# A fused two-layer block: two weight matrices staged in other buffers and loaded later, and one made partly by GpSimd

## The reference

```python
# layer 1, on h = layernorm(x)
h   = rmsnorm(h) * g_res @ W_in + b_in
s   = scan over the context rows: s[i] = a * s[i-1] + c * rmsnorm(ctx[i]) * g_init   # first 512 of 1024 channels
x   = x + h + s[plug]            # plug: one row of s for each token, from the cumulated lengths
# layer 2, on y = layernorm(x)
xr  = mu_r * y + (1 - mu_r) * y_prev ;  xk = mu_k * y + (1 - mu_k) * y_prev
out = x + sigmoid(xr @ W_r.T) * (relu(xk @ W_k.T) ** 2 @ W_v.T)
```

## Time and profile before

| | us |
|---|---|
| median of 3 runs | 780.18 |
| lowest, highest | 779.64, 780.68 |
| profiled execution | 780.35 |
| its span, first to last instruction | 778.8 |
| mean granted TensorE clock | 0.992 |

### The profile page before, as it was taken

How to read it: one execution, slowest core, us unless ns; L and a number is a source line. 1 busy time by engine, 2 the same in 40 slices (tenths; PEclk the granted TensorE clock), 3 DMA queues, 4 the chain that set the end, 5 groups by cost and what they waited for, 6 DMA issues and landing times.

```text
span 778.8 us, 10909 instructions
## 1 busy us (share of the span) xinstructions
PE 755.4 (97%) x3462; PEld 621.9 (80%) x3463; DVE 556.2 (71%) x1005; ACT 413.7 (53%) x682; POOL 175.5 (23%) x175
## 2 busy tenths in 40 slices
PE   7878899999999999999999999999999999999997
PEld 4656688888888888888888888888888888888876
DVE  6797886766858677686776769577676967667552
ACT  4346565554546655455664545556454655544760
POOL 6622131313102131220313122131311213130000
PEclk9999999999999999999999999999999999999999
DMA  8556170524417053350705326071531706140011
GB/s 311 147 192 178 41 215 3 153 105 109 149 42 216 0 128 128 88 169 37 213 7 122 135 69 187 14 194 50 121 135 47 209 0 185 72 108 15 1 54 55
DMA packets 42765, 85.73 MB, mean 110 GB/s; under 512 B 3536, under 2 KB 3536, under 8 KB 42704
## 3 DMA queue, kind: packets, MB, share of 16 engines
q1 hardware_dynamic: 30768, 63.74, 21.8%
q0 software_dynamic: 9216, 16.78, 13.6%
q10 hardware_dynamic: 2736, 4.73, 1.8%
HBM read 64.26 MB, written 21.76 MB: 110 GB/s over the span
## 4 chain that ended last, share of the span: by engine, by line
PE 88%; DVE 4%; DMA 2%; issue 2%; ACT 2%; POOL 1%; SPq 0%; DVEq 0%; ACTq 0%; POOLq 0%
PE bank L494 28%; PE bank L495 28%; PE bank L496 28%; PE bank L599 3%; DMA xt<-in_x_turned 1%; POOL ring L433 1%; DMA s_rows<-scanned 1%; DMA ctx_rows<-in_ctx 1%; DVE ring L1034 1%; DVE xk_lo L908 1%; DVE scratch L1004 0%; DVE gate L1062 0%; ACT scratch L809 0%; DVE bn_a L937 0%; ACT scratch L807 0%
## 5 line engine op out<-in xcount | busy, mean ns | idle before, releaser
L433 POOL DMA_INDIRECT ring<-s_rows,patch_now x60 | 101.7, 1695 | 262.7 <-DMA s_rows<-scanned 231.0
L908 DVE TENSOR_TENSOR xr_lo<-scratch,xr_hi 128x512 fp32r<-128x512 f32 x124 | 85.6, 690 | 70.3 <-ACT xr_hi L715 69.8
L1004 DVE SCALAR_TENSOR_TENSOR scratch<-turned,cols,scratch 128x512 f32<-128x512 f32 x128 | 94.5, 749 | 31.5 <-ACT scratch L764 24.9
L715 ACT ACTIVATE turned<-bank 128x512 f32<-128x512 f32 x64 | 33.2, 604 | 137.1 <-PE bank L599 133.5
L494 PE MATMUL bank<-wi_hi,xt_hi 128*128 128x512 f32 x256 | 102.1, 399 | 3.3 <-DVE xt_lo L908 2.7
L494 PE MATMUL bank<-xk_hi,wk_hi 128*128 128x512 f32 x256 | 100.1, 391 | 3.4 <-DVE xk_lo L908 3.4
L494 PE MATMUL bank<-wr_hi,xr_hi 128*128 128x512 f32 x256 | 99.7, 390 | 1.0 <-DVE xr_lo L908 1.0
L495 PE MATMUL bank<-wi_lo,xt_hi 128*128 128x512 f32 x256 | 100.4, 392 | 0.0
L496 PE MATMUL bank<-wi_hi,xt_lo 128*128 128x512 f32 x256 | 100.2, 391 | 0.0
L496 PE MATMUL bank<-xk_hi,wk_lo 128*128 128x512 f32 x256 | 99.6, 389 | 0.0
L495 PE MATMUL bank<-xk_lo,wk_hi 128*128 128x512 f32 x256 | 99.6, 389 | 0.0
(11 more groups left out here) (134 smaller groups left out, 1283.4 us busy)
## 6 DMA issues: line engine op xcount, KB each, us to landing
ring<-in_x SPq DMA_DIRECT2D x16, 1024.0 KB, 7.4
out<-gate SPq DMA_DIRECT2D x64, 256.0 KB, 2.1
xt<-in_x_turned SPq DMA_DIRECT2D x14, 1024.0 KB, 5.2
ctx_rows<-in_ctx SPq DMA_DIRECT2D x16, 512.0 KB, 8.0
s_rows<-scanned ACTq DMA_DIRECT2D x16, 256.0 KB, 2.4
gate<-in_L_xattn_W_in SPq DMA_DIRECT2D x4, 256.0 KB, 6.2
xt<-in_x_turned SPq DMA_DIRECT2D x2, 512.0 KB, 8.0
ring<-in_x_turned SPq DMA_DIRECT2D x1, 1024.0 KB, 12.9
```

Source lines behind the costliest of these rows:

```text
L433: pool.indirect_dma_start(ring[b.slot][:, t, :], None, s_rows[:, :], bass.IndirectOffsetOnAxis(ap=rows, axis=0), compute_op=ALU.add).then_ ...
L715: return nc.scalar.activation(to, of, ACT.Copy)
L908: return nc.vector.tensor_tensor(to, whole, high, ALU.subtract)
L1004: nc.vector.scalar_tensor_tensor(scratch[:, 2 + i % 2, :], turned[:, c, 1:S + 1], cols[:, 1 + which, c:c + 1], scratch[:, i % 2, :], ALU.m ...
```

## The change

Edits on five engines, all in the opening:

- Staging: W_r into `xt`, W_k into `gate`, W_v into ring buffer 2.
- SP: W_r is loaded once x_lo(0) is whole, W_k once `s_stored` of batch 0 has come, ahead of batch 1's context, and W_v once `s_stored` of batch 1 has come. Guards of the shared buffers follow.
- GpSimd: low parts 0 to 2 of W_k after `root_c(1)`, part 3 after `root_b(0)`; `root_a(1)` ahead of batch 1's gathers; the identity matrix made earlier.
- PE: the first scan after chunk 0 of the first projection; the gate product waits for W_r's low parts one by one.
- ACT: W_k's high parts in iteration -1, ahead of `squares_c(1)`; in iteration 0 `gates` ahead of W_v's high parts, and `squares_c(2)` after `squares(0)`. Two small loads are issued after the averages.
- DVE: no W_k; W_r's low parts between the mixes; `x_lo(1, 1)`, `stats_c(1)` and `scan_input(1)` inside the loop of sums; `norm_b(1)` between `ka_low(0, 1)` and `ka_low(0, 2)`.

```diff
-        staged = [gate, turned[:, :, 1:S + 1], ring[2], gate]
+        staged = [gate, xt, gate, ring[2]]
...
+            reached(sp, xt_lo_ready, Batch(0, 0), 2, 2)
             load_w(WR, w_r)
+
+            reached(sp, s_stored, Batch(0, 0), 16, 16)
+            sp.wait_ge(w_lo_ready[WIN], C)
+            load_w(WK, w_k)
 
             reached(sp, far_over, Batch(0, 0), 1, 1)
             load_ctx(Batch(0, 1))
             rows_added(sp, Batch(0, 0))
             load_x(Batch(0, 1))
-
+            reached(sp, s_stored, Batch(0, 1), 16, 16)
             reached(sp, xt_lo_ready, Batch(0, 1), 2, 2)
-            load_w(WK, w_k)
-            sp.wait_ge(w_lo_ready[WIN], C)
             load_w(WV, w_v)
...
                     reached(sp, xt_lo_ready, new.plus(-1), 2, 2)
+                    if is_first(new, 2):
+                        sp.wait_ge(w_lo_ready[WR], C)
                     load_xt(new)
                     reached(sp, out_ready, b.plus(-1), T, T)
                     if is_first(new, 2):
-                        sp.wait_ge(w_lo_ready[WK], C)
+                        sp.wait_ge(w_lo_ready[WV], C)
                     load_x(new)
...
+            def weight_lo(w, first, last):      # GpSimd
+                for c in range(first, last):
+                    pool.wait_ge(w_hi_ready[w], c + 1)
+                    nc.gpsimd.tensor_tensor(wt_lo[w][:, c, :], staged[w][:, c, :], f32(wt_hi[w][:, c, :]),
+                                            ALU.subtract).then_inc(w_lo_ready[w], 1)
...
+                if is_first(nxt):
+                    weight_lo(WK, C - 1, C)
                 if new.exists(B):
                     far(new)
+                    if is_first(nxt):
+                        root_a(new)
                     add_patches(new)
-                if is_first(nxt):
-                    root_a(new)
...
             root_c(Batch(0, 1))
+            weight_lo(WK, 0, C - 1)
             batches(pool, iteration, B)
...
-                            pe.wait_ge(w_lo_ready[WR], C)
+                            pe.wait_ge(w_lo_ready[WR], c + 1)
...
                 for t in range(T):
                     project_tile(Batch(0, 0), t, c)
-                    if c == 1 and t == 1:
-                        pe.wait_ge(decay_lo_ready, 1)
-                        scan(Batch(0, 0))
                 if c == 0:
                     sum_marks()
+                    pe.wait_ge(decay_lo_ready, 1)
+                    scan(Batch(0, 0))
...
-                        act.wait_ge(w_lo_ready[WV], C)
+                        act.wait_ge(w_lo_ready[WK], C)
...
                     elif is_first(b):                 # ACT, iteration 0
                         mix_hi(b, 0, C)
-                        weight_hi(WK)
                         mix_hi(b, C, 2 * C)
+                        gates(b)
                         weight_hi(WV)
-                        gates(b)
-                        squares_c(new)
...
                 if is_first(b):
                     squares(b)
+                    squares_c(new)
                     u_high(new)
...
                 if is_first(nxt):                     # ACT, iteration -1
                     x_hi(new, 1)
+                    weight_hi(WK)
                     squares_c(new)
...
                 if is_first(nxt):                     # DVE, iteration -1
-                    stats_c(new)
                     for t in range(T):
                         add_x(nxt, t)
                         statistics_b(nxt, t)
+                        if t == 1:
+                            x_lo(new, 1)
+                            stats_c(new)
+                        if t == 2:
+                            scan_input(new)
                     stats_b(nxt, T)
-                    scan_input(new)
                     u_low(new)
                     norm_b(nxt)
+                    weight_lo(WR, 0, 1)
                     scan_out(new)
...
-                if b.exists(B):                       # DVE, iteration 0
+                if is_first(b):
+                    mixing(b, 0, 2)
+                    weight_lo(WR, 1, 2)
+                    mixing(b, 2, 3)
+                    weight_lo(WR, 2, 3)
+                    mixing(b, 3, 4)
+                    weight_lo(WR, 3, 4)
+                    mixing(b, 4, 5)
+                elif b.exists(B):
                     mixing(b, C if is_last(b) else 0, 2 * C if is_last(b) else C + 1)
-                if is_first(b):
-                    weight_lo(WK)
...
+                if nxt.exists(B):
+                    add_x(nxt, 3)
                 if is_first(b):
                     weight_lo(WV)
                 if nxt.exists(B):
-                    add_x(nxt, 3)
                     stats_b(nxt)
                 if is_first(b):
                     ka_low(b, 0)
+                    ka_low(b, 1)
+                    norm_b(nxt)
+                    ka_low(b, 2)
+                    ka_low(b, 3)
                     stats_c(new)
-                    ka_low(b, 1)
                     scan_input(new)
-                    ka_low(b, 2)
                     stats_a(new)
-                    ka_low(b, 3)
                     u_low(new)
-                    norm_b(nxt)
...
-            x_lo(Batch(0, 0), 0)                      # DVE, ahead of the iterations
             dve.wait_ge(cols_loaded, 16)
             dve.wait_ge(w_averaged, 1)
             centre(0)
             centre(1)
+            x_lo(Batch(0, 0), 0)
...
             u_low(Batch(0, 0))
+            x_lo(Batch(0, 0), 1)
             weight_lo(WIN, 2, 3)
             dve.wait_ge(bias_loaded, 16)
             scan_out(Batch(0, 0))
             patches()
-            statistics_a(Batch(0, 0), 0)
-            x_lo(Batch(0, 0), 1)
             weight_lo(WIN, 3, 4)
-            stats_a(Batch(0, 0), 1)
+            stats_a(Batch(0, 0))
...
             x_lo(Batch(0, 1), 0)
-            weight_lo(WR, 0, 2)
-            x_lo(Batch(0, 1), 1)
-            weight_lo(WR, 2, C)
             batches(dve, iteration, B)
```

More of the change, by code:

```diff
@@ L459, in iteration @@
                     root_c(new)
+                if is_first(nxt):
+                    weight_lo(WK, C - 1, C)
                 if new.exists(B):
                     far(new)
+                    if is_first(nxt):
+                        root_a(new)
                     add_patches(new)
-                if is_first(nxt):
-                    root_a(new)
             make_decay(0, P, 0)
             make_blocks()
+            nc.gpsimd.memset(ident[:, :], 0.0).then_inc(ident_ready, 1)
+            pool.wait_ge(ident_ready, 1)
+            nc.gpsimd.affine_select(out=ident[:, :], in_=ident[:, :], compare_op=ALU.not_equal, fill=1.0, base=0,
+                                    pattern=[[-1, P]], channel_multiplier=1).then_inc(ident_ready, 1)
             pool.wait_ge(half_ready, 1)
@@ L471, in _ @@
             make_decay(1, W32, P)
-            nc.gpsimd.memset(ident[:, :], 0.0).then_inc(ident_ready, 1)
-            pool.wait_ge(ident_ready, 1)
-            nc.gpsimd.affine_select(out=ident[:, :], in_=ident[:, :], compare_op=ALU.not_equal, fill=1.0, base=0,
-                                    pattern=[[-1, P]], channel_multiplier=1).then_inc(ident_ready, 1)
             pool.wait_ge(patches_ready, 1)
@@ L818, in turned_out @@
                         reached(act, mix_lo_ready, b.plus(-1), 2 * C, 2 * C)
-                        if is_first(b):
-                            act.wait_ge(w_lo_ready[WR], C)
                     copy(turned[:, :, 1 + t * P:1 + (t + 1) * P],
@@ L869, in _ @@
             nc.scalar.activation(v_b[:, 0, :], average[:, 0:1], ACT.Copy).then_inc(table_loaded, 1)
-            act.dma_start(g_ctx[:, :], g_init[0:D].partition_broadcast(P)).then_inc(g_ctx_loaded, 16)
-            act.dma_start(bias[:, :], b_in.partition_broadcast(P)).then_inc(bias_loaded, 16)
             act.wait_ge(cols_loaded, 16)
@@ L874, in _ @@
                 nc.scalar.activation(averages[:, c, :], average[:, :], ACT.Copy, scale=cols[:, 0, c:c + 1]).then_inc(averages_ready, 1)
+            act.dma_start(g_ctx[:, :], g_init[0:D].partition_broadcast(P)).then_inc(g_ctx_loaded, 16)
+            act.dma_start(bias[:, :], b_in.partition_broadcast(P)).then_inc(bias_loaded, 16)
             x_hi(Batch(0, 0), 0)
@@ L1084, in iteration @@
                     return
-                if b.exists(B):
+                if is_first(b):
[7 more added lines that the diff above has]
+                elif b.exists(B):
                     mixing(b, C if is_last(b) else 0, 2 * C if is_last(b) else C + 1)
-                if is_first(b):
-                    weight_lo(WK)
                 if nxt.exists(B):
```

## The result

The changed kernel takes 781.84 us (median of 10 runs, 780.09 to 782.55), the kernel before 779.62 (10 runs, 778.87 to 780.68): a ratio of 1.0029, 95% interval 1.0018 to 1.0039. It is 2.2 us slower, where I had forecast 777.3 and at most 780.9. The profiled execution after took 781.74 (span 780.2), the one before 780.35 (span 778.8): 1.4 apart, the other 0.8 because the one before was itself 0.7 above its median.

A forecast was written before the change was run, and what follows sets the result against it. PE bounds the kernel and never idles from 100 us on, so only the opening counts: scan(2) starting 3.0 us earlier, 86.2 against 89.23, takes 780.35 to 777.35 (777.2 against the median), said as 777.3; range 774.8 to 780.9.

The forecast's parts named there:

- u_low(2) is late next: Ahead of scan(2): u_low ends at 86.1 behind stats_a(2), so scan(2) starts at 86.2 against 89.23, 3.0 us earlier.
- sums 0 to 2 are done as their gathers land, and sum 3 starts at 40.9: DVE in batch 0: only gather 3, landing at 40.8, holds the last sum, and the normalization starts at 44.6, 1.3 earlier.
- 0.4 of a bound of 3.9: Batch 0's gathers: W_k's load beside them delays gather 3 by 0.4 us, from a possible 0 to 3.9.
- The store behind W_r: Batch 0's store, issued at about 22.2, lands with W_r at 26.0, where alone it would land in 2.4 us.
- the 2 us are gone: Batch 0's gathers begin at 26.9 against 27.13, although the store is issued some 2 us earlier.
- GpSimd's low parts: Three of W_k's after root_c(1) at 37.8, 1.5 us each, end at 42.3, hidden ahead of root_b at 43.2.
- adds two sums: DVE among the mixes for batch 1: sums come between mixes 4 and 5, and mix 7 ends at 65.1.
- From the gates to scan(2): Gates end at 69.1, chunk 2 of the value product starts at 79.0, scan(2) at 86.2.
- The slower case: GpSimd's low parts of W_k take up to 3.1 us each, delaying root_b(0): 781.2, or 782.9 with the clock; chance 0.1.
- nothing comes through: W_k beside batch 0's gathers costs the 3.9 us bound less the 0.4 taken, on gather 3: 780.3; chance 0.08.
- The clock falls behind scan(2): PE's 1.7 us at the lower clock falls after its wait for scan(2), leaving 1.3 of gain: 779.0; chance 0.2.

The follow-up runs named there:

- e1: The changed kernel with only chunk 0 of W_k loaded, 256 KB in place of 1 MB: 781.00 us.
- e2: The changed kernel with x_lo(1, 1) moved ahead of DVE's loop of sums: 780.82 us.
- e12: e8 with W_k loaded behind batch 0's gathers again, its low parts on DVE behind the first five mixes: 774.53 us.
- e7: e4 with W_r in its own buffer, loaded with the first loads, its low parts on DVE ahead of the sums: 777.97 us.
- e4: The changed kernel with x_lo(1, 1) and all four low parts of W_k on DVE ahead of its sums, none on GpSimd: 781.31 us.
- e9: The changed kernel with W_r alone put back: own buffer, loaded with the first loads, low parts on DVE ahead of batch 0's sums: 780.38 us.
- e3: The changed kernel with GpSimd's fourth low part of W_k made only after batch 0's whole normalization: 781.84 us.
- e5: The changed kernel with two DVE orders of iteration 0 turned, stats_b(1) ahead of W_v's low parts and u_low(2) ahead of stats_a(2): 778.28 us.
- e10: e8 with only chunk 0 of W_k loaded: 774.80 us.
- e11: The kernel before with only the edits ahead of the iterations, not where W_r, W_k and W_v are loaded: 778.58 us.
- e8: e7 with the two turned DVE orders of e5: 773.98 us, ratio 0.9928 to the kernel before.

## Why the prediction was wrong

The mechanism (follow PE to scan(2); u_low(2) is late next) was right, the times up to it were not: scan(2) at 90.25, not 86.2. Where the 4.05 us arose:

| point | forecast | trace after | late by |
|---|---|---|---|
| store (0) issued, landed | 22.2, 26.0 | 23.19, 27.2 | 1.2 |
| gather 0 begins | 26.9 | 28.11 | 1.2 |
| sum 3 | 40.9 | 43.02 | 2.1 |
| normalization | 44.6 | 47.02 | 2.4 |
| first mix | 51.4 | 54.42 | 3.0 |
| batch 1's gathers | 53.6 | 56.78 | 3.2 |
| gates over | 69.1 | 73.24 | 4.1 |
| chunk 2 | 79.0 | 83.51 | 4.5 |
| scan(2) | 86.2 | 90.25 | 4.05 |

- **The step that failed**: "sums 0 to 2 are done as their gathers land, and sum 3 starts at 40.9". I charged W_k's load to gather 3 alone (0.4 of a bound of 3.9), which it did not delay: 40.4. It delayed gather 0, from some 5 to 8.4 us. I had hung nothing on gather 0, yet behind it stand 6.4 us of DVE that can't start earlier: 36.6 + 6.4 = 43.0. By the forecast's own 26.9 + 5.0 and that row the answer would have been 38.3, hidden; with 8.4 for the gather it is 41.7, 0.8 late, and the store's 1.2 makes up the rest. e1 shows that the load stretches the gather, e2 that x_lo(1, 1) is 1.1 of the row, e12 that with a short row the last gathers decide.
- **The store behind W_r** was right in kind: it landed 0.6 behind W_r (issued 21.25, 5.3). But I took its 26.0 as a small loss ("the 2 us are gone") and did not ask what undoing it is worth. e7 against e4: 3.3 us, and e9: 1.5. Of the 1.2 by which gather 0 was later, 0.35 was W_r's issue, 0.2 its landing and 0.6 the store behind it. That the store itself was issued 1.0 late (DVE waited 0.63 for PE, whose clock was 0.50 from 16 to 20 us) did not count: in e3 it was issued at 22.15, and gather 0 began at 28.30.
- **GpSimd's low parts**: the price came out right (1.4 against 1.5; 1.27 where DVE is not in the way), in part by luck, the place wrong, since root_c(1) came at 40.72 and not before 37.8, and I had no term for what they do to DVE: v_b 0.27 longer, scan_input 0.4, the normalization 0.95. That is the step from 2.1 to 3.0 in the table, and e3 shows that it goes when the part is moved. The prediction said that no row showed its size and then took it for nothing. The luck: I took four times the 0.386 us of 128 columns, but the same instruction with 32 columns takes 0.288 on average in the kernel before, so most of the 0.386 doesn't grow with the columns; by these two rows 512 columns of one operand are an estimated 0.8 us, and two operands 1.6 at most.
- **Batch 1**: later by what batch 0 was, and by part of a wait of 1.64 of the second sum for its gather (0.9 more by the time the gates are over). I had "adds two sums" without a wait.
- **From the gates to scan(2)**: each step took what was forecast (gates over to chunk 2: 10.3 against 9.9; chunk 2 to scan(2) 6.7 against 7.2). The prediction listed stats_b(1) behind W_v's low parts and stats_a(2) ahead of u_low as terms of the sum. It followed the order as written and got right what it costs: e5 took 3.6 us out by turning both.
- **The rivals.** The slower case had GpSimd's parts at 2.8 us or more; it came out slower by another way. The nearest was "nothing comes through", in which W_k costs up to 3.9 beside the gathers; it had a chance of 0.08, hung on gather 3, and gave 780.3. "The clock falls behind scan(2)" is not in the profiled execution after, but in those of e1, e3 and e4. The runs of the changed kernel have a median granted clock of 0.988, the 31 of the kernel before beside e1 to e4 have 0.993, so some of its executions may have it or a longer low stretch at 40.63; which one is open, since only one was profiled.

How much W_k's load costs in the changed kernel was not taken apart fully: e1 gives 0.8, not clear of noise and with a store that landed 1.4 later in the profiled execution, and e10 can't tell. Put together, the change lost on W_r (late), on GpSimd's parts, on W_k beside gather 0 with x_lo(1, 1) behind it, and on the order of iteration 0, while its setup gained (e11). W_v behind batch 1's store gained too by the traces (batch 1's gathers begin at 51.48 in e8, at 53.19 in e11), but was not run by itself. e8 keeps these two gains and W_k's early load, loads W_r with the first loads again, makes every low part on DVE ahead of the sums, and turns the two orders.

## What to carry to other kernels

When a bulk load is put beside several small dependent transfers, ask what it does to the first of them and how much work stands in order behind it, not only whether the last one still lands in time. Moving the load of a weight from a slack place to one ahead of a store that everything waits for costs whatever the store is held for, and what an engine gains by offloading shrinks where the other engine's instructions stop it. Where the sum says "X is late next", try the reordering that takes X out before anything else: here moving two blocks of calls was worth 3.6 us.

## What the runs showed of the hardware

- **GpSimd and DVE stop each other, an instruction at a time.** Timelines of the kernel after, cut to single instructions; first GpSimd's first and second low part:

```profile
41.28 1.27 POOL L441 TENSOR_TENSOR wk_lo<-gate,wk_hi 128x512 fp32r<-128x512 f32 x1
...
42.51 1.73 POOL L441 TENSOR_TENSOR wk_lo<-gate,wk_hi 128x512 fp32r<-128x512 f32 x1
```

then the first of the four normalizations:

```profile
47.02 1.50 DVE L1068 TENSOR_SCALAR normed<-ring,mv_b,rs_b 128x512 f32<-128x512 f32 x1 [0.92 <-POOL rs_b L407]
```

  scan_input began at 41.94 and ended at 43.09, 0.5 behind the end of the low part it met (42.55), and the next low part took 1.73 and not 1.27. The first normalization, 0.54 alone, ended 0.3 behind the low part beside it (46.95 + 1.28 = 48.23). v_b, 0.17 alone, ended at 45.50, that part at 45.48. The sums (one input in PSUM, 0.74) and the statistics (0.69) beside low parts kept their time. This is what the Trainium skill (SBUF — State Buffer, section SBUF: two separate sides) states: the port pair that the two engines share is an exclusive lock, held for a whole instruction, which DVE needs for two SBUF inputs or in its two-port mode. The trace agrees, with waits of 0.27 to 0.96 us.
- **A small store behind a large load**: batch 0's 256 KB landed in 4.0 to 6.3 us in the seven kernels in which W_r's megabyte had been issued 1.2 to 2.2 us ahead of it, against 2.0 to 3.8 where W_r was among the first loads and the median of 2.5 in the changed kernel.
- **A gather beside a 1 MB load and a context** landed in 8.4 and 7.4 us (the first two), 5.6 and 5.3 (the last two); in the kernel before, without the megabyte, the four took 5.0, 5.2, 6.4 and 5.8.
- **The spread of one kernel goes with the clock**: 31 runs of the kernel before on one chip lay between 777.34 and 781.30; the six fastest had a mean granted clock of 0.997 or 0.998, the six slowest 0.989 to 0.992. It is no strict order: the run with the lowest clock, 0.985, took 780.34.
